# Second pass of a two-layer ViT tower: norm, gates and mixture moved to earlier steps

## What is computed

```python
# _L1_attn: bottleneck of 96, two Mamba directions, normed, added, projected up
h = x @ down_W + down_b
fwd = _ln(_mamba(h, f_...), f_ln_g, f_ln_b)
bwd = _ln(_mamba(h[:, ::-1], b_...), b_ln_g, b_ln_b)
return (fwd + bwd[:, ::-1]) @ up_W + up_b
# the scan in _mamba: 192 features, 16 states
dA = exp(dt_t[:, :, None] * A); h = dA * h + (dt_t * u_t)[:, :, None] * B_t[:, None, :]
y = (h * C_t[:, None, :]).sum(-1)
# _L1_ffn: linear experts, top 2 of 8 by softmax
probs = softmax(x @ router_w.T + router_b); top_probs, ids = top_k(probs, 2)
w = top_probs / (sum(top_probs) + 1e-9)
out = sum_k w_k * (x @ expert_w[ids_k].T + expert_b[ids_k])
```

## Time and profile before

| | |
|---|---|
| median of 3 runs | 966.21 us (961.38 to 966.85) |
| the profiled execution | 961.01 us |
| its span, first to last instruction | 959.2 us |
| mean granted TensorE clock, of full speed | 0.89 |
| busy: TensorE, VectorE, ScalarE, GpSimd | 741.7, 564.3, 403.8, 395.1 us |
| second pass: first scan to the end of the last | 541.0 to 892.75 us |

### The profile page before, as it was taken

One profiled execution on the slowest core, in us unless ns is written; L12 is line 12 of the kernel. 1 busy time (PEld: TensorE's weight loads), 2 busy tenths in 40 slices (PEclk: granted clock), 3 DMA queues, 4 the chain that ended last, 5 costly groups with the idle time before them and its releaser, 6 DMA issues. The chain is left out here.

```text
span 959.2 us, 11504 instructions
## 1 busy us (share of the span) xinstructions
PE 741.7 (77%) x3608; PEld 587.3 (61%) x3608; DVE 564.3 (59%) x968; ACT 403.8 (42%) x876; POOL 395.1 (41%) x311
## 2 busy tenths in 40 slices
PE   7877887784647879887999568797769986986756
PEld 5645656553437879787899346565556764663534
DVE  4167779679675613312112587888877787789320
ACT  1548374282225224322345356373617352733110
POOL 1045745665663321321003244653538333834503
PEclk8899999797667989999999789988978999897978
DMA  9469655355585567877676778697688657967211
GB/s 349 134 211 337 206 158 143 100 148 145 144 232 150 164 193 237 262 234 232 212 232 191 196 195 223 173 239 182 153 220 218 153 141 222 240 151 191 79 61 37
DMA packets 84668, 179.51 MB, mean 187 GB/s; under 512 B 12740, under 2 KB 32832, under 8 KB 83840
## 3 DMA queue, kind: packets, MB, share of 16 engines
q1 hardware_dynamic: 79776, 171.55, 63.3%
q0 software_dynamic: 4832, 7.24, 2.6%
HBM read 158.02 MB, written 20.69 MB: 186 GB/s over the span
## 5 line engine op out<-in xcount | busy, mean ns | idle before, releaser
L1670 PE MATMUL PS<-PR,CM 128*128 128x304 f32 (+1 forms) x672 | 186.3, 419 | 92.7 <-POOL PR L790 63.8
L790 POOL TENSOR_TENSOR PR<-ST,V 128x608 f32<-128x608 f32 x96 | 142.3, 1482 | 185.7 <-DVE ST L1304 155.5
L1670 PEld LDWEIGHTS PS<-PR,CM 128*128 128x128 f32 x672 | 126.5, 220 | 135.7 <-POOL PR L790 77.7
L956 ACT ACTIVATE dA<-dA,negA 128x304 f32<-128x304 f32 x192 | 93.6, 538 | 151.8 <-DMA BB<-rows_d 151.7
L1304 DVE TENSOR_TENSOR_SCAN ST<-dA,PS 128x608 f32<-128x608 f32 x96 | 136.3, 1420 | 15.1 <-ACT dA L956 10.9
L1008 ACT ACTIVATE HID<-PS,WX 128x128 f32<-128x128 f32 x204 | 59.5, 367 | 149.7 <-PE PS L1670 147.6
L703 POOL TENSOR_TENSOR dA<-dA,aP 128x607 f32<-128x607 f32 x48 | 70.7, 1475 | 73.1 <-ACT aP L976 71.2
L1293 DVE TENSOR_TENSOR PS<-BB,PS 128x608 f32<-128x608 f32 x96 | 76.2, 794 | 22.5 <-DMA BB<-rows_d 11.3
L1500 DVE TENSOR_TENSOR xp<-PS,WXB 128x192 f32<-128x192 f32 x34 | 12.2, 358 | 128.2 <-PE PS L1670 123.4
L1670 PE MATMUL PS<-XT,WX 128*128 128x128 f32 x408 | 84.1, 290 | 1.0 <-ACT HID L1008 1.0
L1670 PE MATMUL PS<-XT,WXR 128*128 128x128 f32 x408 | 83.8, 289 | 0.0
(11 more groups left out here) (363 smaller groups left out, 1287.8 us busy)
## 6 DMA issues: line engine op xcount, KB each, us to landing
dA<-rows_d SPq DMA_DIRECT2D x144, 304.0 KB
BB<-rows_d SPq DMA_DIRECT2D x144, 304.0 KB
WX<-ex_m SPq DMA_DIRECT2D x34, 576.0 KB
WX<-ex_m SPq DMA_DIRECT2D x34, 387.0 KB, 3.8
slots_d<-WXR SPq DMA_DIRECT2D x8, 960.0 KB, 8.2
WXR<-ex_r SPq DMA_DIRECT2D x34, 192.0 KB, 4.6
WX<-gates_d SPq DMA_DIRECT2D x4, 1216.0 KB, 6.3
CM<-c SPq DMA_DIRECT2D x1, 4430.0 KB, 19.6
```

Of the source, the lines that this page charges most:

```text
L790: nc.gpsimd.tensor_tensor(PRq[:, c % 2], STq[:, c % 2], DIRS[k].Cw.unsqueeze(1).broadcast_to([128, QB, T]), ALU.mult).then_inc(q_product.s ...
L956: last = nc.scalar.activation(dAq[:, slot, i, :], dAq[:, slot, i, :], ACT.Exp, scale=negA[:, j:j + 1])
L1670: return nc.tensor.matmul(out, lhsT, rhs, start=first, stop=last)
```

## The change

Operations of the second pass get other places in the lists; none is added or left out. By engine:

- SP: in `part_b`'s row reads, `write_gates` follows row read 9 and `read_gates` row read 10, where they stood behind row read 11, on both sides of `write_rows`; `load_next` one row read earlier.
- GpSimd: the first two of the six `gate_inputs` of a group move to steps 10 and 11 of its B half (`MIX_EARLY`), the other four to steps 0 to 3 of the A half.
- ScalarE: in A, `rstd` of `tail` at step 10, `rstd` of `nxt` and the `logits` copy at step 11 (they stood at A 11, B 0 and B 2); in B, `inputs` at step 2 (3), `ratio` at 3 (5).
- VectorE: in A, `add_mixture` at step 5 (7), `output_residual` at 7, in front of `steps` (8), `expert_residual` and `centre` at 8 (9), `scale` at 10 and `scale_down` at 11 (both B 0); in B, `gates_top` at 1 (3), `find_rows` at 2 (3), `gates_weights` at 3 (5), `gates_rows` at 5 (7).
- TensorE: `mixture` part 0 at the end of B, the others at A 0 to 4 (1 to 6); the up-projection at A 6 (7), `back` at 7 (8), `variance` of `tail` at 9 (10) and of `nxt` at 10 (11) with `project_down`, `logits` at A 11 (B 1); in B, `direction_out` and `direction_var` at 2 and 3 (1 and 2), `logits_T` at 0 (2), `gates_T` at 4 (6).

```diff
@@ -26,7 +26,7 @@
 WARM = 24
-MIX_PARTS, REST_FROM, REST_PARTS = 6, QSTEPS - 3, 3
+MIX_PARTS, MIX_EARLY, REST_FROM, REST_PARTS = 6, 2, QSTEPS - 3, 3
 EXPERTS, FFN = 8, 768
@@ -664,18 +664,18 @@
                     read_rows(g, 1, c)
-                    if c == 4 and g + 2 < GROUPS:
+                    if c == 3 and g + 2 < GROUPS:
                         load_next(g + 1)
+                    if c == 9 and g:
+                        write_gates(g - 1)
+                    if c == 10 and g:
+                        read_gates(g - 1)
                     if c == 8 and g >= 2:
...
                         store_end(g - 2)
-                if g:
-                    write_gates(g - 1)
                 if g + 1 < GROUPS:
                     write_rows(g + 1, 0)
-                if g:
-                    read_gates(g - 1)
             store(GROUPS - 2)
@@ -806,8 +806,8 @@
                         gather(0, range(TILES))
-                    if mix is not None and n < MIX_PARTS:
-                        gate_inputs(mix, n)
+                    if mix is not None and n + MIX_EARLY < MIX_PARTS:
+                        gate_inputs(mix, n + MIX_EARLY)
                     if nxt == 0 and n in IN_PART_A:
@@ -823,6 +823,8 @@
                         gather(far, (n - 4,))
+                    if tail is not None and n >= QSTEPS - MIX_EARLY:
+                        gate_inputs(tail, n - (QSTEPS - MIX_EARLY))
                     if nxt == 0 and n in IN_PART_B:
@@ -1084,16 +1086,22 @@
                             step_logs(g, 1)
-                    if n == 7 and mix is not None:
+                    if n == 5 and mix is not None:
                         act.wait_ge(out_free.sem, out_free.after(mix, 1))
                         nc.scalar.activation(Or[:, :], Q.Hr[:, :], ACT.Copy).then_inc(rest_copied.sem, 1)
-                    if n == 10 and tail is not None:
+                    if n == 9 and tail is not None:
                         squares(Q, tail, 0)
-                    if n == 11:
+                    if n == 10:
                         if nxt is not None:
...
                             rstd(Q, tail, Q_BANK)
+                    if n == 11:
+                        if nxt is not None:
+                            rstd(L, nxt, L_BANK)
+                        if tail is not None:
+                            logits(Q, tail, Q_BANK, cm("er_b", p=EXPERTS))
+                            nc.scalar.activation(Q.XrK[DR:128, :], Q.Xr, ACT.Copy).then_inc(x_doubled.sem, 1)
                     if nxt == 0 and n in IN_PART_A:
@@ -1104,26 +1112,20 @@
                     if nxt is not None and n == 0:
-                        rstd(L, nxt, L_BANK)
-                    if nxt is not None and n == 1:
                         act.wait_ge(L.ln_x.sem, L.ln_x.after(nxt, 1))
...
                     if n == 2:
-                        if tail is not None:
-                            logits(Q, tail, Q_BANK, cm("er_b", p=EXPERTS))
-                            nc.scalar.activation(Q.XrK[DR:128, :], Q.Xr, ACT.Copy).then_inc(x_doubled.sem, 1)
                         if g is not None:
                             output(g, 0, tail)
-                    if n == 3:
-                        if g is not None:
-                            output_root(g, 0)
                             if nxt is not None:
...
                             inputs(nxt, 0)
-                    if n == 5:
-                        if nxt is not None:
-                            projected(nxt, 0)
+                    if n == 3 and g is not None:
+                        output_root(g, 0)
+                    if n == 5 and nxt is not None:
+                        projected(nxt, 0)
+                    if n == 3:
                         if tail is not None:
@@ -1595,26 +1597,30 @@
                         combine(nxt)
-                    if n == 7 and mix is not None:
+                    if tail is not None:
+                        if n == 1:
+                            gated_output(tail, 1)
+                        if n == 5:
+                            output_norm(tail, 1)
+                        if n == 7:
+                            if mix is not None:
+                                dve.wait_ge(rest_copied.sem, rest_copied.after(mix, 1))
+                            output_residual(tail)
+                    if n == 5 and mix is not None:
                         add_mixture(mix)
...
                         steps(g, 1)
-                    if tail is not None:
-                        if n == 1:
-                            gated_output(tail, 1)
-                        if n == 5:
-                            output_norm(tail, 1)
-                        if n == 8:
-                            if mix is not None:
-                                dve.wait_ge(rest_copied.sem, rest_copied.after(mix, 1))
-                            output_residual(tail)
-                    if n == 9:
+                    if n == 8:
                         if nxt is not None:
...
                             centre(Q, Q, tail, 0, Q_BANK)
+                    if n == 10 and tail is not None:
+                        scale(Q, tail, 0)
+                    if n == 11 and nxt is not None:
+                        scale_down(nxt)
                     if n == 11 and mix is not None and tail is None:
@@ -1625,30 +1631,25 @@
                         direction_step(g, 1, n)
-                    if n == 0:
-                        if nxt is not None:
-                            scale_down(nxt)
-                        if tail is not None:
-                            scale(Q, tail, 0)
-                        if mix is not None:
-                            add_mixture_rest(mix)
-                    if n == 1 and g is not None:
-                        gated_output(g, 0)
-                    if n == 3:
+                    if n == 0 and mix is not None:
+                        add_mixture_rest(mix)
+                    if n == 1:
+                        if g is not None:
+                            gated_output(g, 0)
                         if tail is not None:
...
                             gates_top(Q, tail, Q_BANK)
-                        if far is not None:
-                            find_rows(far)
+                    if n == 2 and far is not None:
+                        find_rows(far)
+                    if n == 3 and tail is not None:
+                        gates_weights(Q, tail)
+                        assert links[Q] == Q.chain.per_group, ("Q", links[Q])
                     if n == 5:
                         if tail is not None:
-                            gates_weights(Q, tail)
-                            assert links[Q] == Q.chain.per_group, ("Q", links[Q])
+                            gates_rows(Q, tail, Q_BANK)
                         if g is not None:
...
                     if n == 7:
-                        if tail is not None:
-                            gates_rows(Q, tail, Q_BANK)
                         if nxt is not None:
@@ -2077,9 +2078,9 @@
                             project_steps(g, 1)
-                    if mix is not None and 0 < n <= MIX_PARTS:
-                        mixture(mix, n - 1)
-                    if n == 7 and tail is not None:
+                    if mix is not None and n + 1 < MIX_PARTS:
+                        mixture(mix, n + 1)
+                    if n == 6 and tail is not None:
                         if mix is not None:
@@ -2088,28 +2089,30 @@
                         last.then_inc(up_proj.sem, 1)
-                    if n == 8:
+                    if n == 7 and nxt is not None:
+                        if g is not None:
+                            pe.wait_ge(dt_raw.sem, dt_raw.after(g, 2))
+                            pe.wait_ge(c_copied.sem, c_copied.after(g, 2))
+                        pe.wait_ge(mixed.sem, mixed.after(nxt, TILES))
+                        if nxt == 0:
+                            pe.wait_ge(gelu_ready.sem, gelu_ready.after(HALF_BLOCKS, 0))
+                            pe.wait_ge(xtok_copied.sem, xtok_copied.after(GROUPS, 0))
+                        back(M, nxt, L_BANK, X_BANK)
+                    if n == 8 and tail is not None:
+                        pe.wait_ge(Q.residual.sem, Q.residual.after(tail, 1))
+                        mean(Q, Q, tail, 0, Q_BANK)
+                    if n == 9:
                         if nxt is not None:
-                            if g is not None:
-                                pe.wait_ge(dt_raw.sem, dt_raw.after(g, 2))
-                                pe.wait_ge(c_copied.sem, c_copied.after(g, 2))
-                            pe.wait_ge(mixed.sem, mixed.after(nxt, TILES))
-                            if nxt == 0:
-                                pe.wait_ge(gelu_ready.sem, gelu_ready.after(HALF_BLOCKS, 0))
-                                pe.wait_ge(xtok_copied.sem, xtok_copied.after(GROUPS, 0))
-                            back(M, nxt, L_BANK, X_BANK)
```

(24 more changed lines are left out.)

## The result

The changed kernel takes 971.0 us (median of 20 runs, 964.8 to 977.9), the kernel before 963.25 (20 runs, 957.5 to 971.1): ratio 1.0073, 95% interval 1.005 to 1.0095. So it is slower by 0.7%, where 0.6% faster was forecast.

A forecast was written before the change was run, and what follows sets the result against it. VectorE's own pace was taken as the floor (96 steps 227 us, 351.8 taken), with waits and small operations between. Terms -7.1+0+1.6-1.2+3.6+1.0-3.9 = -6.0 against the median 966.2 gave 960.2 us; range 946 to 969.

The forecast's parts named there:

- The waits in front of A2 and A3: First rows of groups 2 and 3's forward halves: waits of 0.6 and 3.6 us replace 5.7 and 5.6, -7.1 us.
- Gates in B1 and B2: Backward halves of groups 1 and 2: the logits wait goes, a ratio wait of 3 to 4 us replaces it, 0 together.
- Its bound of -7 for a ratio in time: Backward halves of groups 1 and 2: if the ratio came in time, -7 us for both together.
- A2 and A3: End of groups 2 and 3's forward halves: TensorE sets it, mean() leaves and logits() enters, -0.6 us each.
- A1: End of group 1's forward half: rstd behind the decay +0.95 and later steps() +0.7, together +1.6 us.
- B3 and behind it: Last backward half: late row read 11 +3.6, ratio +1.0; after the last scan, earlier up-projection -3.9 us.
- The slower rival: SP's queue: gate read holds row read 11 and row writes by 7.4 us in every group; +11.4, 977.6 us, chance 0.10.

The follow-up runs named there:

- second profile: The changed kernel run once more, unaltered, to see how far two profiles agree: ratio 1.0073 to the kernel before.
- ratio first: Changed kernel with ScalarE's ratio and shift at B step 2, ahead of output, inputs and output_root: 0.9957 and, repeated, 0.9977 to the kernel before.
- variance first: Changed kernel with ScalarE's rstd(Q) ahead of the decay at A step 10 and TensorE's variance(Q) ahead of step 8's sum: 1.0087 to the kernel before.
- the read in its old place and the ratio late: Changed kernel with gate write and read behind row read 11, all gate products and mixture parts in the A half: 1.0133 to the kernel before.
- the filler: ratio first plus 28 unread TensorE products at A step 9: 0.9977 to the kernel before; with gate reads also issued by ScalarE, 0.9942.
- read as before, ratio first: the read in its old place, with ScalarE's ratio ahead of output, inputs and output_root: 1.0032 to the kernel before.

## Why the forecast was wrong

**The waits in front of A2 and A3: right, and then partly given back.** From the end of scan 5 in B2 (787.6) the read was issued 5.7 us later (4.8 forecast), the row writes 9.9 (10), done 18.5 (17.9), the first scan started 24.2 (23.8); waits 0.7 and 3.7 where 0.6 and 3.6 were forecast. (The 17.9 should be 18.2 by its own figures, 467 KB at 2.46 us for 608 behind T+16.3.) In the second profile A3's wait is 3.6 again, but A2's 3.2, so the 0.6 came out in one profile of two. SP's timeline shows B2: first write to first row read 8.5 us, against 4.6 unhindered.

```profile
793.29 0.33 SPq L642 DMA_DIRECT2D WX<-gates_d  x1
...
797.54 0.33 SPq L621 DMA_DIRECT2D rows_d<-q_DL  x1
...
806.09 0.55 SPq L510 DMA_DIRECT2D dA<-rows_d  x1
```

Yet B1 and B2 won 2.7 us instead of 7.1. Of the 4.4, 1.4 is A2's wait, as the mean of 0.7 and 3.2, and 0.8 lies between scans 8 and 11 of the two. The largest part, 2.1, is lost in B1 at steps() (from scan 7 to scan 8 it takes 9.5 us in both profiles, 7.4 before), which I had not looked at again. Counted from the end of scan 5, VectorE comes there 3.1 us sooner and GpSimd with its gathers only 0.6, so two of VectorE's operations lie beside GpSimd's products and take 2.1 and 2.4 us (before: one, 2.28; alone 0.43 and 0.63). VectorE in B1 before, then VectorE and GpSimd in the changed B1:

```profile
695.68 2.28 DVE L1359 SCALAR_TENSOR_TENSOR q_DL<-q_DL,q_OM 128x456 f32<-128x456 f32 x1
```
```profile
694.00 2.14 DVE L1357 TENSOR_SCALAR q_TM<-q_OM 128x456 f32<-128x456 f32 x1 [0.51 <-ACT q_OM L945]
...
697.51 0.65 DVE L1361 SCALAR_TENSOR_TENSOR q_DL<-q_DL,q_OM 128x456 f32<-128x456 f32 x1
698.19 2.40 DVE L1362 TENSOR_TENSOR q_WV<-q_DL,q_UP 128x456 f32<-128x456 f32 x1
```
```profile
694.40 1.48 POOL L790 TENSOR_TENSOR PR<-ST,V 128x608 f32<-128x608 f32 x1
...
698.60 1.49 POOL L790 TENSOR_TENSOR PR<-ST,V 128x608 f32<-128x608 f32 x1
```

They end 0.3 and 0.5 us after the product. The Trainium skill (SBUF — State Buffer, section Terms) has VectorE and GpSimd share a pair of SBUF ports, locked for a whole instruction, and the loser blocked. The rows agree in that VectorE's operations end just behind the product, but VectorE's start first, by 0.4 us; that this is the cause wasn't tried.

**Gates in B1 and B2: right.** From scan 1 to the scan of step 6 it is 22.1 us in B1 (22.9 before) and 21.9 in B2 (21.2): 0 together, as forecast. Its bound of -7 for a ratio in time is near what ratio first shows: 20.0 and 18.4 us, together 5.8 less than before.

**A2 and A3: the step that failed.** "I take -0.6 each", because TensorE sets the end; measured +1.6 and +3.2. That TensorE sets the end is confirmed: behind its pause it runs without a gap to the end of both halves, and with variance first the wait for q_RS is gone and nothing gained (53.9 and 48.9; 52.2 and 49.9 in the changed kernel, mean of two). But the size came from counting products (mean out, logits in), and two things lie elsewhere.

The larger one is at the front of A3, which the forecast put at nothing: from its first scan to scan 5 it takes 17.1 and 16.9 us instead of 14.9, 2.1 of the 3.2. ScalarE's decay of row 4 starts 54.6 us behind scan 1 of B2 in both profiles, before the change 53.2, although the first row came 0.7 to 0.9 sooner; scan 5 waits 3.8 and 3.6 us for ScalarE, which has inputs() behind that row (2.3 before). VectorE's timeline, before and changed:

```profile
828.60 1.42 DVE L1304 TENSOR_TENSOR_SCAN ST<-dA,PS 128x608 f32<-128x608 f32 x1 [2.31 <-ACT dA L956]
```
```profile
828.95 1.42 DVE L1306 TENSOR_TENSOR_SCAN ST<-dA,PS 128x608 f32<-128x608 f32 x1 [3.79 <-ACT dA L958]
```

With the read in its old place and the ratio late, A3 starts 1.5 to 1.8 later and takes 15.4: scan 5 lies 61.8 us behind scan 1 of B2 in all three (46.4+15.4, 44.7+17.1, 44.9+16.9; 60.4 in the kernel before); with ratio first it is 58.4 with the old read and 57.1 and 58.6 with the early one. So the earlier start of A3 is worth nothing by scan 5, but for one profile. Why the rows then land at 2.3 to 3.4 us each, and not at 2.2 as before, is open: from 816 to 822 us the DMA engines are full in both, and move 253 to 258 GB/s (first profile) against 279 to 293.

The smaller one is behind steps(): in A3 TensorE, its mean done, pauses 4.8 us (2.7 before) and restarts at 1.2 GHz. TensorE's timeline, before and changed:

```profile
844.46 0.78 PE L1670 MATMUL PS<-q_Hm,ones_d 128*128 128x304 f32 x2 [2.72 <-DVE q_Hr L1562]
```
```profile
845.63 2.39 PE L1671 MATMUL PS<-PR,CM 128*128 128x152 f32 x8 [4.83 <-POOL PR L790]
```

The 0.7 us that A3 lost there came back with the filler. What A2 lost, about 0.7 between scans 5 and 8 and 0.4 to 1.5 behind them, didn't; as the filler itself cost 1.9 there, whether the clock is the cause stays open.

**A1: +1.6 forecast, +0.6.** steps() gives the 0.7 forecast; the rstd behind the decay is no later than the wait it replaces (17.7 us from scan 8 to scan 1 of B1, 17.8 before).

**B3 and behind it: +0.7 forecast, +5.1.** Here the mis-sized term is the landing. I took 9.1 us from read to GpSimd's product out of a stretch without row reads the earlier trace rows. Among them it took 12.15 and 9.52 in the two profiles, 9.3 to 12.4 in the variants with the read ahead of row read 11. From the end of scan 5 in B3:

| us | gates read | gates there | last scan starts | up-projection |
|---|---|---|---|---|
| forecast | 4.8 | 13.9 | 17.3 | 29.3 |
| changed, two profiles | 5.3, 6.0 | 17.4, 15.5 | 19.8, 18.5 | 34.0, 31.7 |
| ratio first, two profiles | 5.7, 5.7 | 15.1, 15.0 | 18.2, 18.1 | 32.5, 32.5 |
| read as before, ratio first | 10.3 | 19.4 | 13.3 | 30.2 |

A read issued 4 to 5 us sooner brings the gates only 2 to 4.4 sooner, and the last scan comes 5 to 6.5 later; the up-projection, which needs both, is later. GpSimd's timeline shows the other end of it: an early gate product done, then a pause for the last scan, where before all six ran without one.

```profile
898.07 1.46 POOL L798 TENSOR_TENSOR WX<-WX,q_Xm 128x608 f32<-128x608 f32 x1 [3.55 <-DMA WX<-gates_d]
901.93 1.46 POOL L790 TENSOR_TENSOR PR<-ST,V 128x608 f32<-128x608 f32 x1 [2.40 <-DVE ST L1306]
903.35 4.33 POOL L798 TENSOR_TENSOR WX<-WX,q_Xm 128x608 f32<-128x608 f32 x3
```

**The rivals.** The slower rival had B3 at +7, which came true (+7.1), but put the rest into B1 and B2, which won; its sum, +11.4, is no better. The misses: 4.4 in B1 and B2, 6.0 in A2 and A3, 4.4 from B3 on, less 1.0 in A1 and 0.9 in A0 and B0; but for rounding they are the 12.9 us between -6.0 and +6.9.

## What to carry to other kernels

A wait that vanishes is worth what is left of it at the next place where another engine's list or the DMA sets the pace: follow each gain through the whole next half (here to scan 5 of A3 and steps() of B1) before it enters the sum. A transfer drawn forward among others takes time from them and can land later after its issue than it did alone (here 9.3 to 13.2 us instead of 9.1); price it with the duration beside them, on whichever of two queues it is. When a chain is drawn forward, put the small operation that others wait for (here the ratio) ahead of the long ones (table loads, a root that waits for TensorE): that one order was worth as much as the whole change lost.

## What the runs showed of the hardware

In B3 a read of 1.8 MB took 9.0 to 9.1 us from issue to its consumer when it was issued 5 us behind the last row read, and 9.3 to 13.2 closer to row reads, in one kernel 12.15 and 9.52. A VectorE operation of 0.63 us beside a GpSimd product took up to 2.40. After a pause of 4.8 us TensorE ran 4 us at a granted clock of 0.50; with products that fill the pause, at 1.00. These products ran 1.3 to 1.9 us past the pause and so took back half of what the clock gave, or all of it.
